# An AdaLN transformer layer: weights of the modulation loaded as plain f32 from the hardware queues, LayerNorm statistics moved ahead of a barrier

## The reference

```python
mod = (_silu(L0_c) @ L0_wmod).reshape(8, 6, 1, -1)       # wmod: 1024 x 6144, f32
sa, ca, ga, sb, cb, gb = (mod[:, i] for i in range(6))   # ga, gb clamped away from 0
h = _layernorm(x) * (1 + ca) + sa
x = x + ga * attention(h)         # 16 heads of 64, causal, relative-position bias, Wq Wk Wv Wo
h = _layernorm(x) * (1 + cb) + sb
x = x + gb * ternary_ffn(h)       # h quantised per row to int8 steps (127 / max|h|),
                                  # weights unpacked from 2-bit codes, 1024 x 1024
```

## Time and profile before

| | us |
|---|---|
| median of 2 timed runs | 1341.56 (1341.14 to 1341.98) |
| the profiled execution, its own time | 1352.13 |
| span of its slowest core (core 5) | 1350.4 |
| spans of its eight cores | 1324.2 to 1350.4 |
| busy on core 5: PE, DVE, ACT, POOL | 776.8, 529.5, 429.5, 136.7 |

### The profile page before, as it was taken

How to read it: one execution, slowest core, us unless ns; L and a number is a source line. 1 busy time by engine, 2 the same in 40 slices (tenths; PEclk the granted TensorE clock), 3 DMA queues, 4 the chain that set the end, 5 groups by cost and what they waited for, 6 DMA issues and landing times.

```text
span 1350.4 us, 16455 instructions; the slowest of 8 cores (1324.2 to 1350.4 us)
## 1 busy us (share of the span) xinstructions
PE 776.8 (58%) x3853; PEld 315.2 (23%) x3853; DVE 529.5 (39%) x1308; ACT 429.5 (32%) x849; POOL 136.7 (10%) x238
## 2 busy tenths in 40 slices
PE   0303504409897878878887887974995001111198
PEld 0001200004343333334333333421331000000043
DVE  0056600034233342433334243342453575444466
ACT  0003300011646546354654735374001013333300
POOL 0112211101111112121111100000000220000000
PEclk9999999999798888889788888977886555555588
DMA  9631137732101111110111100000000000000023
GB/s 294 195 69 15 21 69 250 237 54 39 12 8 28 11 28 13 25 14 8 29 11 28 14 17 1 2 17 17 0 0 13 20 0 0 1 0 0 1 109 140
DMA packets 47923, 61.11 MB, mean 45 GB/s; under 512 B 33389, under 2 KB 38573, under 8 KB 44760
## 3 DMA queue, kind: packets, MB, share of 16 engines
q0 software_dynamic: 32352, 33.59, 12.0%
q1 hardware_dynamic: 13102, 24.85, 6.0%
q10 hardware_dynamic: 2378, 1.64, 0.5%
HBM read 58.31 MB, written 10.14 MB: 51 GB/s over the span
## 4 chain that ended last, share of the span: by engine, by line
PE 50%; DMA 18%; DVE 15%; issue 9%; ACT 6%; DVEq 1%; SPq 0%; ACTq 0%; POOL 0%; POOLq 0%
PE p_o L721 15%; PE p_s L613 8%; PE p_s L682 6%; PE p_s L784 5%; DMA swm<-wm 5%; PE p_v L641 5%; PE p_f L930 5%; DMA swq<-wq 3%; DMA swv<-wv 3%; DMA sx<-x 2%; DMA swk<-wk 2%; DVE soT L591 2%; PE p_v L647 2%; PE p_mod L394 2%; ACT sPt L697 2%
## 5 line engine op out<-in xcount | busy, mean ns | idle before, releaser
L697 ACT ACTIVATE sPt<-p_s 128x512 bf16<-128x512 f32 (+3 forms) x640 | 298.2, 536 | 244.2 <-PE p_s L682 240.7
L721 PE MATMUL p_o<-sPt,sv 128*65 128x512 bf16 (+3 forms) x640 | 228.9, 405 | 95.5 <-DVE soT L755 36.0
L911 PE MATMUL p_tr<-sid,sy 128*128 128x128 bf16 x128 | 25.0, 271 | 214.1 <-DVE sy L906 195.0
L682 PE MATMUL p_s<-sqt,skt 64*128 64x512 bf16 (+3 forms) x640 | 124.6, 401 | 7.1 <-DVE skt L620 7.1
L652 DVE CAST sv<-p_v 128x128 bf16<-128x128 f32 x128 | 37.7, 294 | 231.9 <-PE p_v L647 231.9
L721 PEld LDWEIGHTS p_o<-sPt,sv 128*65 128x65 bf16 x640 | 66.0, 116 | 222.2 <-issue 213.8
L394 PE MATMUL p_mod<-swm,scsil 128*1 128x512 f32 x96 | 44.7, 617 | 87.2 <-DMA swm<-wm 87.2
L641 PE MATMUL p_v<-swv,shT 128*128 128x128 bf16 x1024 | 85.0, 230 | 0.0
L784 PE MATMUL p_s<-swo,soT 128*128 128x512 bf16 x256 | 72.4, 435 | 15.5 <-DVE soT L591 15.5
L705 DVE TENSOR_TENSOR sPt<-sPt,sE 128x240 bf16<-128x240 bf16 (+1 forms) x256 | 61.3, 266 | 39.0 <-ACT sPt L697 34.7
L641 PEld LDWEIGHTS p_v<-swv,shT 128*128 128x128 bf16 x1024 | 71.5, 103 | 14.6 <-issue 6.4
(11 more groups left out here) (101 smaller groups left out, 769.4 us busy)
## 6 DMA issues: line engine op xcount, KB each, us to landing
swm<-wm POOLq DMA_DIRECT2D x24, 1024.0 KB, 6.1
sx<-x SPq DMA_DIRECT2D x16, 512.0 KB
out<-sx SPq DMA_DIRECT2D x16, 512.0 KB
srbt<-dsumB SPq DMA_DIRECT2D x16, 256.0 KB
swq<-wq POOLq DMA_DIRECT2D x64, 32.0 KB, 2.1
swk<-wk POOLq DMA_DIRECT2D x64, 32.0 KB, 2.1
swv<-wv POOLq DMA_DIRECT2D x64, 32.0 KB, 2.1
swo<-wo POOLq DMA_DIRECT2D x8, 256.0 KB, 3.7
```

The source lines that it names most:

```text
L682: o=o, qc=qc: e.matmul(pb[:, qoff:512], skt[o:o + 64, 128 * kt:128 * (kt + 1)], sqt[o:o + 64, 512 * qc + qoff:512 * (qc + 1)], start=True, ...
L697: hb=hb: e.activation(sPt[:, sl, hb, qoff:512], pb[:, qoff:512], AF.Exp, bias=EXPB, scale=F1),
L721: sl=sl, nkt=nkt, vb=vb: e.matmul(p_o2[hb][:, qoff:512], sv[:, vb, kt, 65 * hb:65 * hb + 65], sPt[:, sl, hb, qoff:512], start=(kt == 0), s ...
```

## The change

Four edits.

1. `swm` and `scsil` are F32 in place of F32R (float32r), so the 96 matmuls of the three `mod_group`s take plain f32 operands.
2. The DMAs of `mod_group` are issued from ACT (groups 0 and 2) and SP (group 1), no longer from POOL. Their places in the list of steps stay.
3. The LayerNorm statistics of stage 3 are taken in the output projection, for each tile after its second half, and `ln_batch` follows before the barrier. In stage 3 the 8 `unpack_chunk`s stand alone ahead of the loop over tiles.
4. The tags `kap` and `qsc`, one for all tiles, become one for each tile.

```diff
-        scsil = sb("scsil", [128, 8], F32R)
+        scsil = sb("scsil", [128, 8], F32)
...
-            swm = sb1("swm", [128, 2, 2048], F32R)
+            swm = sb1("swm", [128, 2, 2048], F32)
...
             def mod_group(jg):
+                qe = ("scalar", "sync", "scalar")[jg]
                 for c in range(NCH):
                     p = (NCH * jg + c) % 2
-                    sq.add("gpsimd", lambda e, jg=jg, c=c, p=p: e.dma_start(
+                    sq.add(qe, lambda e, jg=jg, c=c, p=p: e.dma_start(
                         out=swm[:, p, :],
...
                         sx[:, t, 512 * half:512 * (half + 1)], p_s[2][:]),
                         reads=["ps:2"], writes=[f"x:{t}"])
+                if half == 1:
+                    ln_stats(t)
+
+            ln_batch()
 
         sq.barrier()
...
-            for t in range(NT):
-                ln_stats(t)
-                if t % 2 == 1:
-                    unpack_chunk(t // 2)
-            ln_batch()
+            for c in range(NCH):
+                unpack_chunk(c)
...
-                    reads=[f"t1:{b}", "swb"], writes=["kap"])
+                    reads=[f"t1:{b}", "swb"], writes=[f"kap:{t}"])
...
-                    reads=[f"t1b:{b}"], writes=["qsc"])
+                    reads=[f"t1b:{b}"], writes=[f"qsc:{t}"])
...
-                    reads=[f"sh2:{b}", "qsc"], writes=[f"st32:{b}"])
+                    reads=[f"sh2:{b}", f"qsc:{t}"], writes=[f"st32:{b}"])
...
-                        reads=[pt, "kap", "gbiast"], writes=["pg3"])
+                        reads=[pt, f"kap:{t}", "gbiast"], writes=["pg3"])
```

## The result

The changed kernel takes 1353.7 us (median of 11 runs, 1350.4 to 1369.9), the kernel before beside it 1340.5 (10 runs). The ratio is 1.0118, with a 95% interval of 1.0084 to 1.0151: 1.2% slower, where 1318 us, 1.7% faster, was forecast. The profiled execution took 1369.9, 16 above the median; its slowest core is core 7, span 1368.3 us. Two cores of the kernel before show the same (649 and 650 us at 0.84). The diff doesn't touch attention, so that part is left out of what follows.

What follows compares the result with a forecast made beforehand. It took serial chains to bound stages 1 and 3, and PE the output projection. Edit 3's -21.7 us and stage 1's -1.5, taken from the median 1341.6, gave 1318 us; range 1304 to 1356.

Steps and rivals of the forecast that it cites:

- Cost 0 for tiles 0 to 14: Output projection: statistics of 1.7 us a tile fit in DVE's 2.16 us of idle time, so these tiles add nothing.
- 6 us as the upper bound: Output projection: if PE ran at 2.4 GHz, DVE's 4.7 us against about 4.3 costs 0.4 a tile, 6 us.
- statistics not hidden: Rival, output projection: DVE becomes the bound, 1324 us, or 1345 if every tile waits for all its statistics; chance 0.06.
- POOL's eight multiplies hide under DVE's 25.7: Stage 3 unpacking: POOL's 16.94 us of multiplies fit beside DVE's 25.7 us for eight chunks, part of the -21.7 us.
- The exposed tail of 4.5 us: End of output projection: the last tile's statistics and `ln_batch` delay the barrier, row loads and `spk` loads by 4.5 us.
- First matmul of group 0 at 43.4: Stage 1: group 0's first two chunk loads, now on ACT, make its first matmul 4.1 us later than before.
- Four passes for f32: Modulation matmuls in stage 1: f32 takes four passes, so a chunk costs PE 6.85 us at 1.2 GHz, 3.45 at 2.4.
- The clock stays up after chunk 0: Stage 1 groups: PE's clock rises in the first chunk and stays; chunk 0 takes 5.2 us, the others 3.45.
- The load times, 6.8 us in group 0 and 5.8 after: Stage 1: DMA time per pair of chunks, giving a pair cadence of 10.8 us in group 0, 9.6 in the others.
- they meet: Stage 1: ACT finishes the odd heads at about 219 us, as group 1's first row copy comes due at 218.5.
- The 219 for the end of the odd heads: Stage 1, ACT: begun at 173.3, three heads are done before the chunks flow, the other five at about 219 us.
- The low-clock rival: Rival, stage 1: PE's clock does not rise or falls in gaps; +38.5 us there, 1358 in all; chance 0.25, part or always.

## Why the prediction was wrong

- **"Cost 0 for tiles 0 to 14" and "6 us as the upper bound".** Wrong, +10. The pace of 2.58 us a half was read on core 5, the slowest core of that execution, which with core 4 ran the projection at 0.83, 81 to 82 us. The other six ran it at nearly full clock in 70 to 72, 4.3 us a tile, and there DVE has about 1.06 us a tile to spare for statistics of 1.7. The bound was too low as well: a tile costs DVE 4.96 us, not 4.7, since every short gap between its instructions counts once it is the bound, and 16 x 0.66 makes the 10 us where 16 x 0.4 had made 6. The rival "statistics not hidden" had 1324 for it.
- **"POOL's eight multiplies hide under DVE's 25.7."** Wrong, and the largest single term: 37.5 us instead of 25.7 from first unpacking to first tile, 11.8 us, and 1.7 in the first tile of the loop. The interleaving that the edit undid had put POOL's multiply beside statistics, which don't touch what POOL needs. I looked at the durations of both and not at what runs beside what.
- **The exposed tail of 4.5 us.** Right, 4.9.
- **First matmul of group 0 at 43.4.** Near: 41.7 after, 42.8 with edits 1 and 2 alone, 3.2 and 4.3 us later than before (38.5 on the median core), forecast 4.1.
- **Four passes for f32.** Right: two instructions of 0.43 us at the high clock, 0.86 a matmul.
- **The clock stays up after chunk 0.** Half right. PE is busy for 30 to 38 us a group where 27.5 would do at 2.4 GHz and 55 at 1.2. It fell again in every group, not in the first chunk alone.
- **The load times, 6.8 us in group 0 and 5.8 after.** Wrong, and the reason that stage 1 lost 10 us instead of gaining 1.5. Group 2, with nothing beside it, took 35.3 us, forecast 34.9. Group 0 took 46.3 instead of 38.8: the weight loads, of which I wrote "ahead of every need", run beside it through this very change; holding them back gave 6.6 us. Edit 1 alone has 45.8 without them, so they are not the whole account of the 46.3. Group 1 took 47.9 instead of 37.5: the heads' DMAs had been priced at 2.5 us for the loads and "they meet" for ACT; moving them gave 8.4, the clock's share and ACT's in it. The 219 for the end of the odd heads is also a wrong sum: three heads of 3.6 and five of 7.7 from 173.3 on make 222.6. The last of their DMAs was issued at 223.5 to 242.4.
- **Edit 4 at 0.** Right.

The low-clock rival had the sign right at 1358 and its mechanism in part, but that its number lies near 1353.7 is luck: it had +38.5 us in stage 1, where 8.7 were measured, and kept the whole gain of edit 3. Three errors of 10 to 14 us on the same side were enough. By the table they are 10.9 (projection), 13.5 (block by POOL) and 10.2 (stage 1), with 0.4 of the tail 35 us, which is 1318 to 1353.

## What to carry to other kernels

Before work is moved under another engine, read that engine's pace on all cores: the core that ends last can be the one on which the host engine is slow and the gap looks wide. When two streams are taken apart that had been interleaved, ask what each instruction will now run beside, on the shared ports and in the DMA queues, and price it there. Tags that made independent DMAs wait for one another, with the place of the `spk` loads and of the heads' DMAs, cost more than every edit of this change together (55 us came off with the three); look at the chain before changing what is in it.

## What the runs showed of the hardware

- A DVE integer-to-bf16 `tensor_scalar` of 0.29 us beside a POOL bf16 multiply of 2.2 us took 2.01 us; f32 `bn_stats` beside it took its usual 0.69.
- A plain f32 matmul of 512 columns is two instructions and takes 0.86 us at 2.4 GHz, four times a bf16 one.
- 1 MB loads to SBUF took longer beside streams of small ones: with edits 1 and 2 a group of eight was 6.6 us shorter without the weight loads beside it (group 0) and 8.4 without the heads' DMAs (group 1), with the clock's share in both. Moving eight heads' DMAs from ACT to SP, where they run before the group, was enough to take the second away.
- PE's clock differs between the cores of one execution in the same stage: before the change the output projection ran at 0.83 and 0.82 on cores 4 and 5 (81 and 82 us) and at 0.96 to 0.98 on the other six (70 to 72 us).
